# First tokens' low halves on VectorE, transposed q and k weights in four PSUM banks, and three loads issued from ScalarE's queue

## The reference

```python
x = L0_attn_x                            # 8 x 1024 x 256, float32
xn = layernorm(x)                        # over the last axis
Q, K, V = (einsum('bsd,ed->bse', xn, w) for w in (wq, wk, wv))   # 16 heads of 16
Q, K = rotate(Q), rotate(K)              # even/odd pairs by sin and cos of the position
probs = softmax(causal(Q K^T / sqrt(16)))
s = einsum('bse,de->bsd', probs V, wo)
gate, up = xn wg^T, xn wu^T              # integer weights / 127, 256 -> 768
g = silu((silu(gate) * up) wd^T)         # integer weights / 127, 768 -> 256
out = x + s * g
```

## Time and profile before

| | us |
|---|---|
| median of 3 runs | 1243.72 |
| lowest and highest of them | 1241.35, 1244.28 |
| the profiled execution, its time | 1242.05 |
| the profiled execution, its span | 1240.3 |
| mean granted TensorE clock in it | 0.988 of full speed |

### The profile page before, as it was taken

How to read it: one execution, slowest core, us unless ns; L and a number is a source line. 1 busy time by engine, 2 the same in 40 slices (tenths; PEclk the granted TensorE clock), 3 DMA queues, 4 the chain that set the end, 5 groups by cost and what they waited for, 6 DMA issues and landing times.

```text
span 1240.3 us, 30191 instructions
## 1 busy us (share of the span) xinstructions
PE 1189.3 (96%) x10707; PEld 552.3 (45%) x10707; DVE 1005.2 (81%) x1221; ACT 843.2 (68%) x1062; POOL 603.0 (49%) x935
## 2 busy tenths in 40 slices
PE   5999999999999799999999999999999999999997
PEld 3566565565555233334334433343334433443333
DVE  6666666666678789998999999999999999999943
ACT  4544554554553377778778887888788878887884
POOL 5756656656653122343445444543454345434554
PEclk9999999999999699999999999999999999999998
DMA  9755455455483311331324313333143133331222
GB/s 268 175 164 168 146 161 163 144 167 161 144 190 125 78 44 45 103 89 50 96 75 108 95 45 105 78 95 95 47 123 109 44 95 87 95 95 45 70 70 86
DMA packets 157879, 134.70 MB, mean 109 GB/s; under 512 B 49472, under 2 KB 142144, under 8 KB 157760
## 3 DMA queue, kind: packets, MB, share of 16 engines
q1 hardware_dynamic: 157760, 133.08, 37.9%
HBM read 72.61 MB, written 50.33 MB: 99 GB/s over the span
## 4 chain that ended last, share of the span: by engine, by line
PE 53%; issue 8%; ACT 2%; DMA 2%; DVE 1%; SPq 1%; POOL 0%; ACTq 0%; DVEq 0%; POOLq 0%
PE ps L1325 20%; PE ps L1308 12%; PE ps L765 10%; PE ps L1361 4%; PE ps L773 3%; PE ps L1345 2%; DMA qs<-mp 2%; ACT pr L1237 2%; PE ps L1353 2%; SPq L978 1%; DVE mxp L789 1%; PE ps L1332 1%; ACT ot L1244 0%; POOL mp L1037 0%; DVE yt L1173 0%
## 5 line engine op out<-in xcount | busy, mean ns | idle before, releaser
L789 DVE TENSOR_REDUCE mxp<-ps 128x2 f32<-128x1024 f32 (+2 forms) x576 | 683.4, 1222 | 61.9 <-PE ps L765 33.5
L1237 ACT ACTIVATE pr<-ps 128x1024 f32<-128x1024 f32 x576 | 569.8, 1032 | 170.0 <-PE ps L1308 163.0
L1325 PE MATMUL ps<-pr,vt 128*32 128x512 f32 (+3 forms) x3072 | 314.7, 497 | 1.3 <-ACT ot L1244 0.7
L1047 POOL TENSOR_SCALAR_AFFINE_SELECT pr<-pr 128x256 f32<-128x256 f32 (+1 forms) x448 | 192.9, 451 | 122.8 <-ACT pr L1237 120.3
L1308 PE MATMUL ps<-qs,ks 50*128 50x512 f16 (+3 forms) x1536 | 226.0, 329 | 13.6 <-ACT pr L1237 3.8
L765 PE MATMUL ps<-ks,qs 48*128 48x512 f16 (+2 forms) x1792 | 226.6, 306 | 10.2 <-DVE mxp L789 4.9
L1037 POOL TENSOR_SCALAR mp<-mneg 32x128 f16<-32x128 f32 x32 | 9.2, 289 | 319.0 <-issue 304.9
L1308 PEld LDWEIGHTS ps<-qs,ks 50*128 50x128 f16 x1536 | 64.5, 93 | 212.4 <-issue 204.8
L653 PE MATMUL ps<-xTh,wguT 128*128 128x512 f16 x384 | 145.7, 379 | 0.8 <-ACT vs L543 0.8
L653 PE MATMUL ps<-xTl,wguT 128*128 128x512 f16 x384 | 145.5, 379 | 0.0
L765 PEld LDWEIGHTS ps<-ks,qs 48*128 48x128 f16 x1792 | 81.9, 94 | 138.1 <-issue 119.9
(11 more groups left out here) (101 smaller groups left out, 1294.8 us busy)
## 6 DMA issues: line engine op xcount, KB each, us to landing
v_d<-vs SPq DMA_DIRECT2D x16, 1024.0 KB, 5.2
vt<-v_d SPq DMA_DIRECT2D x32, 512.0 KB, 4.0
xs<-in_L_attn_x SPq DMA_DIRECT2D x16, 512.0 KB, 4.2
q_parts_d<-parts SPq DMA_DIRECT2D x16, 512.0 KB, 3.0
k_parts_d<-parts SPq DMA_DIRECT2D x16, 512.0 KB, 3.1
gate_d<-gs SPq DMA_DIRECT2D x16, 512.0 KB, 3.2
qs<-q_parts_d SPq DMA_DIRECT2D x64, 128.0 KB, 3.1
ks<-k_parts_d SPq DMA_DIRECT2D x64, 128.0 KB, 3.1
```

What stands on the lines that cost most here:

```text
L789: dve.tensor_reduce(dst, ps[:, slot:slot + 2, :].rearrange("p t (n s) -> p (t n) s", s=w), axis=AX.X, op=ALU.max).then_inc(keep["max_dve"] ...
L1047: pool.affine_select(out=blk, in_=blk, compare_op=ALU.is_ge, fill=0.0, base=0, pattern=[[0, 2], [0, len(hs)], [1, P]], channel_multiplier= ...
L1237: act.activation(probs(step, s).rearrange("p (t j) s -> p t j s", t=2)[:, :, hs[0]:hs[-1] + 1, 0:w], ps[:, slot:slot + 2, 0:w * len(hs)].r ...
L1325: ins = pe.matmul(ps[VW * j:VW * (j + 1), O0, lo - c * CH:CH], vt[g % 2][:, kb, j, :], probs(step, s)[:, j, at:at + w], start=first, stop= ...
```

## The change

Five things are done, all of them outside the loop over the middle batches:

- The low halves of the first chunk's tokens are made by DVE, between the small product L387 and the copy L389 of the scale chain; POOL made them before.
- wq and wk are transposed into four PSUM banks, one for each half of the contraction (4, 5 and 6, 7), wv into bank 0 and wo into bank 1, and the maxima go to bank 2. ACT raises a semaphore after each half, so that DVE can begin the low halves of the first half while ACT writes the second.
- DVE's statistics of chunk (0, 1) come behind the low halves of wq and wk; they came ahead of them before.
- Within chunk (0, 0), DVE normalises chunk (0, 1)'s tokens between the rotation of q and that of k; it did so ahead of both. ACT makes wo's high halves and casts the third integer weight ahead of the high halves of chunk (0, 1)'s tokens; it did so behind them. POOL's order in the chunk stays.
- w_gate, w_up and the first half of the rotation table are loaded from ACT's queue, once wv has arrived; before, SP issued them, w_gate and w_up behind the tokens of chunk (0, 1) and the table behind the first two transposes.

```diff
-        W_BANK = (4, 5, 0, 1)
-        MAX_BANK = 7
+        W_BANK = ((4, 5), (6, 7), (0,), (1,))
+        MAX_BANK = 2
...
+            def load_trig(eng, c):
+                for t in range(2):
+                    eng.dma_start(trig[:, t, :, c * CH:(c + 1) * CH], cs[:, t, :, c * CH:(c + 1) * CH]).then_inc(s_trig[c], 16)
@@ block.sync
-                for i, w in enumerate((w_gate, w_up)):
-                    sp.dma_start(rawi[:, MH * i:MH * (i + 1), :], w.rearrange("(m p) d -> p m d", p=P)).then_inc(s_iload[i], 16)
...
                 transpose_tokens(sp, (0, 0))
-                load_trig(0)
...
-                load_trig(1)
+                load_trig(sp, 1)
@@ block.vector
                 def weight_low(i):
-                    dve.wait_ge(s_whi, i + 1)
-                    for hi, lo, src in weight_pieces(i):
-                        ins = dve.scalar_tensor_tensor(out=lo, in0=src, scalar=wscale[:, i:i + 1], in1=hi,
-                                                       op0=ALU.mult, op1=ALU.subtract)
+                    for n in range(len(W_BANK[i])):
+                        dve.wait_ge(s_whi, halves_made(i, n))
+                        for hi, lo, src in weight_pieces(i, n):
+                            ins = dve.scalar_tensor_tensor(out=lo, in0=src, scalar=wscale[:, i:i + 1], in1=hi,
+                                                           op0=ALU.mult, op1=ALU.subtract)
                     ins.then_inc(s_wlo, 1)
...
                 ch(dve.tensor_tensor(diag4[:, :], ident[0:4, 0:4], wmaxT[:, :].to_broadcast([4, 4]), ALU.mult))
+                low_tokens(dve, (0, 0))
                 dve.wait_ge(s_maxT, 2)
...
-                stats(dve, (0, 1))
                 weight_low(0)
                 weight_low(1)
+                stats(dve, (0, 1))
...
                     if more:
                         if not is_first(step):
                             stats(dve, nxt(step))
-                        normalise(dve, nxt(step))
+                            normalise(dve, nxt(step))
                     if is_first(step):
                         weight_low(2)
...
                     rotate(step, 0, q_pe)
+                    if is_first(step):
+                        normalise(dve, nxt(step))
                     peek(step, "k0")
                     rotate(step, 1, k_pe)
@@ block.gpsimd
                 inverse_root(pool, (0, 0))
-                low_tokens(pool, (0, 0))
@@ block.scalar
                 def weight_high(i):
-                    for hi, lo, src in weight_pieces(i):
-                        ins = act.activation(hi, src, ACT.Copy, scale=wscale[:, i:i + 1])
-                    ins.then_inc(s_whi, 1)
+                    for n in range(len(W_BANK[i])):
+                        for hi, lo, src in weight_pieces(i, n):
+                            ins = act.activation(hi, src, ACT.Copy, scale=wscale[:, i:i + 1])
+                        ins.then_inc(s_whi, 1)
...
+                act.wait_ge(s_wload[2], 16)
+                for i, w in enumerate((w_gate, w_up)):
+                    act.dma_start(rawi[:, MH * i:MH * (i + 1), :], w.rearrange("(m p) d -> p m d", p=P)).then_inc(s_iload[i], 16)
+                load_trig(act, 0)
                 high_tokens(act, (0, 0))
...
-                    if more:
-                        high_tokens(act, nxt(step))
                     if is_first(step):
                         weight_high(3)
                         cast_ints(2)
+                    if more:
+                        high_tokens(act, nxt(step))
                     high_part(step, 0)
                     values(step)
```

More of the change, by code:

```diff
@@ L201, in high_tokens, with low_tokens @@
             act.activation(xh[:, :, :], xn[:, :, :], ACT.Copy).then_inc(x_hi.sem, 1)
[L203 to L206, removed]
+        def low_tokens(eng, step):
+            eng.wait_ge(t_lo.sem, t_lo.after(earlier(step, 1)))
+            eng.wait_ge(x_hi.sem, x_hi.after(step))
+            eng.tensor_tensor(xl[:, :, :], xn[:, :, :], xh[:, :, :], ALU.subtract).then_inc(x_lo.sem, 1)
         def transpose_tokens(sp, step):
@@ L236, in project_phase, with weight_pieces, halves_made @@
         wscale = sb("wscale", [P, 4], F32)
-        W_BANK = (4, 5, 0, 1)
-        MAX_BANK = 7
+        W_BANK = ((4, 5), (6, 7), (0,), (1,))
+        MAX_BANK = 2
         SCALED = 6
-        def weight_pieces(i):
+        def weight_pieces(i, n):
             if i < 2:
-                view = lambda kd, eo: ps[:, W_BANK[i], kd * D:(kd + 1) * D].rearrange("p (h i two) -> p two i h", i=PAIRS, two=2)[:, eo]
-                part = lambda hl, kd, eo: wqkT[:, hl, kd, 2 * i + eo, :].rearrange("p (i h) -> p i h", h=H)
-                return [(part(0, kd, eo), part(1, kd, eo), view(kd, eo)) for kd in range(KD) for eo in range(2)]
+                view = lambda eo: ps[:, W_BANK[i][n], 0:D].rearrange("p (h i two) -> p two i h", i=PAIRS, two=2)[:, eo]
+                part = lambda hl, eo: wqkT[:, hl, n, 2 * i + eo, :].rearrange("p (i h) -> p i h", h=H)
+                return [(part(0, eo), part(1, eo), view(eo)) for eo in range(2)]
             w = (wvT if i == 2 else woT)
-            return [(w[:, 0].rearrange("p k e -> p (k e)"), w[:, 1].rearrange("p k e -> p (k e)"), ps[:, W_BANK[i], :])]
+            return [(w[:, 0].rearrange("p k e -> p (k e)"), w[:, 1].rearrange("p k e -> p (k e)"), ps[:, W_BANK[i][n], :])]
+        def halves_made(i, n):
+            return sum(len(W_BANK[j]) for j in range(i)) + n + 1
         qk_dst = [d.rearrange("b (r p) s -> b p r s", p=P) for d in (q_parts_d, k_parts_d)]
@@ L282, in _ @@
                 sp.dma_start(xs[:, 1], x_v[0, 1]).then_inc(x_ld[1].sem, 16)
-                for i, w in enumerate((w_gate, w_up)):
-                    sp.dma_start(rawi[:, MH * i:MH * (i + 1), :], w.rearrange("(m p) d -> p m d", p=P)).then_inc(s_iload[i], 16)
-                def load_trig(c):
-                    for t in range(2):
-                        sp.dma_start(trig[:, t, :, c * CH:(c + 1) * CH], cs[:, t, :, c * CH:(c + 1) * CH]).then_inc(s_trig[c], 16)
                 def transpose_ints(i):
@@ L598, in _ @@
                         for m in range(KD):
-                            o = (kd * KD + m) * P
-                            ins = pe.transpose(ps[:, W_BANK[i], o:o + P], raw[:, 2 * i + m, kd * P:(kd + 1) * P], ident[:, :])
+                            bank, o = (W_BANK[i][kd], m * P) if i < 2 else (W_BANK[i][0], (kd * KD + m) * P)
+                            ins = pe.transpose(ps[:, bank, o:o + P], raw[:, 2 * i + m, kd * P:(kd + 1) * P], ident[:, :])
                     ins.then_inc(s_wt, 1)
```

## The result

| | median us | lowest to highest | runs |
|---|---|---|---|
| before | 1243.24 | 1240.92 to 1244.28 | 11 |
| after | 1246.52 | 1243.66 to 1249.54 | 11 |

The ratio of after to before is 1.0031, with a 95% interval from 1.0021 to 1.0040: 3.9 us slower (2.6 to 5.0); the two medians differ by 3.3 us. The profiled execution's span is 1244.5 us, 4.2 above that of before. The forecast was 1246.6.

A forecast was written before the change was run, and what follows sets the result against it. PE was taken to bound the first phase: starting 1.2 us earlier, then losing 4.1 us to the wait behind POOL, so 2.9 us later. Added to the 1243.72 us median this gave 1246.6 us, range 1243.2 to 1249.8.

The forecast's parts named there:

- The head up to the weights: Before PE's first projection: small product 0.15 us, `xl` on DVE 1.09, scale copy at 12.87, ACT's high halves at 13.74.
- The tokens' transposes: First chunk's transposes on SP's queue: `xTl` issued at 12.95, taking 4.4 us, landing at 17.35 and coming last before PE's start.
- ACT's issues: ACT's four load issues ahead of `xh`: 2.2 to 4.2 us from 7.3 on, ACT taken as free at 10.0, covered by DVE's normalisation.
- The hole: Chunk (0, 0): PE waits 3.2 us ahead of m = 2 for `values`, queued behind the next chunk's tokens.
- the forecast's list: Chunk (0, 0), steps from q's rotation at S + 5.42 through `normalise`, `xh`, `xl`, `rotated(0)` to PE resuming at S + 17.03.
- S: Start of PE's first projection, forecast at 17.5 us, 1.2 us earlier than before.
- the clock falls in the new hole: Rival, chance 0.30: PE's clock drops in chunk (0, 0), costing 1.0 to 1.8 us more, 3.9 to 4.7 in total.
- The sum: Whole kernel: 2.9 us later, span 1243.2 us, and 1246.6 us against the median of the runs.
- S - 14.6: Delay of m = 3 in chunk (0, 0), from S + 19.65 against 34.25 before; 2.9 us later at S = 17.5.
- its own case: Main case, chance 0.51: PE's first projection starts at 16.15 to 18.3 us, making the kernel 1.5 to 3.7 us slower.
- the rival with S at 19: Clock-fall rival (chance 0.30) with PE's first projection starting at 19 us: 6 us slower.
- Other moves cost nothing: Around chunk (0, 0): later statistics and ACT's reordered casts cost nothing; the casts would only if w_down came after 23 us.

The follow-up runs named there:

- e1: Changed kernel with `normalise` of chunk (0, 1) put back ahead of both rotations; ratio to the kernel before 1.0009 (1.0000 to 1.0018).
- e7: Changed kernel with only POOL's order in chunk (0, 0) changed, `low_tokens` behind `rotated(1)`; ratio to the kernel before 1.0028 (1.0015 to 1.0041).
- e8: Kernel before with only w_gate, w_up and the table's first half loaded from ACT's queue; ratio to the kernel before 1.0007 (0.9994 to 1.0020).
- e3: Changed kernel with `normalise` put back and the loads issued by SP again; ratio to the kernel before 1.0003 (0.9993 to 1.0013).
- e2: Changed kernel with w_gate, w_up and the table's first half issued by SP again; ratio to the kernel before 1.0021 (1.0012 to 1.0030).
- e4: Kernel before with only `normalise` of chunk (0, 1) moved between the rotations of q and k; ratio to the kernel before 1.0030 (1.0019 to 1.0040).
- e5: Changed kernel with `normalise`, the loads and ACT's order all put back; ratio to the kernel before 1.0004 (0.9991 to 1.0016).
- e6: Changed kernel with `normalise` and loads put back, and POOL's `low_tokens` behind `rotated(1)` in chunk (0, 0); ratio to the kernel before 0.9999 (0.9986 to 1.0012).
- e9: Changed kernel with `normalise` put back and the table on SP's queue, w_gate and w_up still on ACT's; ratio to the kernel before 1.0010 (0.9998 to 1.0022).

## Why the prediction came out

*The head up to the weights: right.* DVE's product took 0.15 us (0.15 forecast), `xl` on DVE 1.23 (1.09), the copy L391 at 12.84 (12.87 forecast), ACT's high halves at 13.70 (13.74).

*The tokens' transposes: mis-sized.* "I take 4.4 us for `xTl`"; it took 6.1, and PE started at 19.2 instead of 17.5. I had `xTl` take its place between the loads; in fact both transposes moved only when ACT's queue was nearly through. The forecast cited the Trainium skill (DMA: Bandwidth & Descriptors, Queues, rings and completion order) for engines that go round between the queues by packets. From 15.5 us on the trace agrees: 120 packets of SP's queue beside 147 of ACT's. Ahead of that it doesn't: `xTh` waited 4.2 us for its first byte, 1.5 us in the kernel before, and meanwhile only ACT's queue was served. It was 4.2 us in e1, e7 and e8 too, though e7's and e8's transposes were issued at 12.64 and 11.82. Why is open; the trace doesn't show descriptors being written, and transposes may be ready later than their issue says.

*ACT's issues: right.* 2.46 us of issuing (forecast 2.7), through at 9.8, ahead of `xh` at 10.24.

*The hole: right in place, cause and size.* 3.2 us were forecast, ended by `values`; it is 3.00. From q's rotation (23.48) PE's m = 2 is 11.52 us away, by the forecast's list 11.61.

*The clock: two effects that cancel in part.* The forecast took 5.42 us from S to q's rotation; it was 4.28, since the faster matmuls began 2.9 us after the start (22.10) and not 5.4. At the start the level is read from the pace of the matmuls alone: the granted clock of the stretches 18 to 22 stands at 1.00 in this trace, and at 0.50 in 18 to 20 of e3's, where the matmuls come at the same 0.43 us. The rival "the clock falls in the new hole" (chance 0.30) came true as well. The busy times by stretches after, granted clock third from the end:

```profile
32.00:34.00 2.00, 0.01 (x1) 0.00 (x0) 0.00 (x0) 1.02 (x2) 2.00 (x2) 1.00 1.58 128
34.00:36.00 2.00, 1.00 (x4) 0.41 (x5) 1.86 (x1) 2.00 (x4) 1.20 (x1) 0.93 0.53 105
36.00:38.00 2.00, 2.00 (x6) 0.71 (x5) 2.00 (x4) 1.23 (x3) 1.48 (x1) 0.50 0.36 129
38.00:40.00 2.00, 2.00 (x8) 0.81 (x7) 0.83 (x2) 0.75 (x2) 1.77 (x2) 0.72 0.56 199
```

The fall cost eight or nine matmuls 0.21 us each more, some 1.8 us, less the 0.7 us that PE waits ahead of m = 3 in e2 and e4, where the matmuls did not slow down: 1.1 us, within the rival's 1.0 to 1.8. It does not follow every such hole: e2 (2.85) and e4 (2.89) kept the fast matmuls.

*The sum: its form is right, the hit of the total is luck.* S - 14.6 gives 4.6 for the S that came about; less 1.1 for the earlier clock, plus some 1.1 for the later one, 4.6. The mark says 4.3, the chunk (0, 1) begins 4.2 later (48.87 against 44.69), and its hole is 1.07 us instead of 0.76. The forecast's 2.9 is short of this by the transposes. S = 19.2 lies outside the 16.15 to 18.3 of its own case; with the fallen clock, what came about is nearly the rival with S at 19, for which it had 6; 1.1 us of the difference is the earlier clock, which was left out there. That the median came out at 1246.52 against 1246.6 is owed to two things that are no part of the mechanism: the kernel before measured 0.5 us faster than in the three runs that the forecast had, and the medians differ by 3.3 us where the traces differ by 4.2. (Those three runs differed by 2.9 us, not by over 3.)

*"Other moves cost nothing": right here, but only under cover.* In the changed kernel ACT's casting ahead of `xh` is hidden behind the moved `normalise`. Without that cover it costs 1.1 us at the mark (e3 against e5): in e3 w_down had landed only at 22.7, close to the 23 us that the forecast named for this kernel, but `xh` could have started at 23.0.

*Not settled.* From the mark to the end, the traces differ by up to 3.5 us with identical code: 833.4 before (1240.3 - 406.90), 836.9 in e3 (1244.0 - 407.15). The half clock between the phases is part of it: in the stretch 432 to 436 it stands at 1.00 before and at 0.50 in e3. Another part isn't explained: e5 has its full clock back by 432, and still 836.5. This is why e3, e5, e6 and e9 have marks apart by 2.4 us and ratios that cannot be told from each other.

## What to carry to other kernels

Before moving an operation on one engine, look on every other engine at what stands behind its result in program order: POOL's sum and ACT's copy of v did not need the next chunk's tokens at all, yet they were queued behind them. Loads moved to a second queue can get ahead of small urgent transfers that used to be issued ahead of them, and hold them up. Where DVE and POOL both work on SBUF, a short operation on the critical chain can last as long as the long one beside it, so place the long one where the chain is through.

## What the runs showed of the hardware

- Transposes on SP's queue moved their first byte 4.2 us after their issue while ACT's queue had 2.5 MB under way (issued 11.40, first bytes after 15.5); without loads on ACT's queue it was 1.5 us (11.45, 12.96), with w_up ahead of them on their own. Then both queues moved about as many packets each (120 and 147), small ones against large ones.
- A DVE operation with SBUF operands and one of POOL held each other up in both directions. On DVE 0.15 us became 2.06 and 1.38 became 3.41 beside POOL's `TENSOR_TENSOR`, 0.17 became 1.78 and 1.38 became 2.82 beside its `MEMSET`; POOL's 2.35 became 3.21. The Trainium skill (GPSIMD Engine Reference, Key points) names contention on SBUF interfaces that the two share, for DVE instructions in a two-port mode or with two SBUF inputs. For two SBUF inputs beside POOL's `TENSOR_TENSOR` the traces agree, down to an operation on 4x4; whether `normalise` and L395, with one such tensor, run in that mode, no run shows.
- It is not every DVE operation. In the kernel before, two on one column took 0.15 and 0.16 us beside POOL's memset of 18.84 to 20.65 (L398 at 19.37, L400 at 19.56, the latter with two SBUF inputs), and in e6 the four products of the rotation, with an operand in PSUM, took 4.60 us, the last two of them beside POOL's sum (from 26.15 on); in the changed kernel two took 2.35 with POOL idle.
- The length of a hole did not decide whether the clock fell: behind those of 2.10 (e9) and 3.00 us (the changed kernel) it stood at 0.50 for a while, behind those of 2.85 (e2) and 2.89 us (e4) it stayed at 1.00.
